# Count stage of a graph network: a block's four fixed tiles get their keys from one 512-column instruction, and their weights from another

## What is computed

```
src, dst = (edge_index[0], edge_index[1])
agg = x + segment_sum(x[src], tgt, num_segments=n)          # layer 0, both directions
h = relu(concat([x_row, x_col - x_row]) @ W1 + b1) @ W2 + b2  # layer 1, segment_max over row
...
comb = dst * num_rel + edge_type                              # layer 3
cnt = segment_sum(ones, comb)
norm = 1.0 / clip(cnt[comb], 1.0)
agg = segment_sum(msg * norm[:, None], dst, num_segments=num_nodes)
```

## Time and profile before

| | us |
|---|---|
| median of 3 runs | 5897.77 (5896.78 to 5898.04) |
| the profiled execution, its own time | 5894.55 |
| span of its core in the trace | 5892.6 |
| count stage, 60 to 731 us of the span | 671 |
| VectorE busy in that stage | 641.5 |
| ScalarE busy in that stage | 269.0 |

### The profile page before, as it was taken

The page is one execution under the profiler, slowest core; times in us unless marked ns, Lnnn a source line. Parts: engine busy times, 40 slices in busy tenths (PEclk is TensorE's granted clock), DMA queues, the critical chain, the costliest instruction groups (busy, mean ns, idle before and its releaser), DMA issues. The chain is left out here.

```text
span 5892.6 us, 107675 instructions
## 1 busy us (share of the span) xinstructions
PE 4004.4 (68%) x31282; PEld 3016.9 (51%) x31283; DVE 3825.4 (65%) x9916; ACT 2230.1 (38%) x2892; POOL 1396.0 (24%) x1703
## 2 busy tenths in 40 slices
PE   4666676635445554445558888888888788878886
PEld 2222276624444444444444444444444488867886
DVE  7999967755655555656534555535555677767776
ACT  2444332001111111111115655545555466646664
POOL 0000000037777777777740000000000000000000
PEclk8999988855555555555558999979999799978998
DMA  1111144522222222222111111111111111111110
GB/s 45 58 67 56 65 175 171 215 61 59 59 59 59 59 59 58 64 58 54 48 33 62 56 56 57 49 51 56 56 56 56 51 46 44 39 36 61 39 44 23
DMA packets 235223, 370.66 MB, mean 63 GB/s; under 512 B 169839, under 2 KB 175973, under 8 KB 235142
## 3 DMA queue, kind: packets, MB, share of 16 engines
q1 hardware_dynamic: 190006, 264.11, 13.8%
q0 software_dynamic: 41536, 85.08, 5.4%
q10 hardware_dynamic: 3600, 20.48, 0.8%
HBM read 292.58 MB, written 76.99 MB: 63 GB/s over the span
## 5 line engine op out<-in xcount | busy, mean ns | idle before, releaser
L1069 POOL DMA_INDIRECT en_got<-edge_q,en_now x1296 | 1302.1, 1005 | 409.4 <-issue 325.1
L1258 PE MATMUL en_t<-ident,en_got 128*128 128x128 f32 x1296 | 361.4, 435 | 957.7 <-DVE en_got L1152 957.7
L1296 ACT ACTIVATE en_hid<-en_t 128x512 f32<-128x512 f32 x324 | 193.5, 597 | 1649.6 <-DMA en_got<-edge_q,en_now 1408.2
L1258 PEld LDWEIGHTS en_t<-ident,en_got 128*128 128x128 f32 x1296 | 231.9, 217 | 1036.1 <-DVE en_got L1152 1036.1
L1266 PEld LDWEIGHTS en_o<-en_w2s,en_hid 128*128 128x128 f32 x2592 | 583.0, 334 | 0.0
L1266 PE MATMUL en_o<-en_w2s,en_hid 128*128 128x64 f32 x2592 | 577.6, 411 | 0.0
L1152 DVE TENSOR_TENSOR en_got<-en_got,p (+1 forms) x324 | 224.5, 693 | 494.7 <-ACTq L1290 462.4
L1855 PE MATMUL r1s_ps<-hp,r1s_count 128*128 128x193 bf16 x5000 | 445.8, 253 | 81.2 <-DVE r1s_count L1807 57.0
L1855 PE MATMUL r0s_ps<-hp,r0s_count 128*128 128x193 bf16 x5000 | 445.6, 253 | 81.4 <-DVE r0s_count L1807 56.2
L456 PE MATMUL cnt_ps<-cnt_hot_l,cnt_hot_k 128*128 128x400 bf16 x1600 | 359.6, 356 | 193.9 <-DVE cnt_hot_l L421 182.0
L1855 PEld LDWEIGHTS r1s_ps<-hp,r1s_count 128*128 128x128 bf16 x5000 | 432.4, 100 | 94.5 <-issue 91.1
(11 more groups left out here) (393 smaller groups left out, 7633.3 us busy)
## 6 DMA issues: line engine op xcount, KB each, us to landing
en_got<-edge_q,en_now POOLq DMA_INDIRECT x1296
count_panels<-cnt_panel SPq DMA_DIRECT2D x25, 800.0 KB, 3.4
type_panels<-cnt_panel SPq DMA_DIRECT2D x25, 800.0 KB, 4.8
c0s_panel<-count_panels SPq DMA_DIRECT2D x25, 800.0 KB, 4.3
count_rows<-c0s_rows ACTq DMA_DIRECT2D x25, 800.0 KB, 3.5
c1s_panel<-count_panels SPq DMA_DIRECT2D x25, 800.0 KB, 5.5
c1s_rows<-count_rows SPq DMA_DIRECT2D x25, 800.0 KB, 7.3
en_raw<-count_panels SPq DMA_DIRECT2D x25, 800.0 KB
```

The costliest lines, as they stand in the source:

```text
L1069: pool.indirect_dma_start(out=got[:, i, j, :], out_offset=None, in_=k.q[:, :], in_offset=bass.IndirectOffsetOnAxis(ap=now[i][:, j:j + 1], ...
L1258: last = pe.transpose(tps[i % 2][:, j * P:(j + 1) * P], got[:, i, j, :], k.ident[:, :])
L1296: act.activation(hid[i % 2][:, :], tps[i % 2][:, :], ACT.Relu).then_inc(lined, 1)
```

## The change

The keys of a block's four fixed tiles are made by one `tensor_tensor` (128 x 4 x 128: `here`, repeated four times, compared with each tile's number from `now`, spread over 128 columns), and their weights by a second (the keys just made, times each tile's power from `now`). Both stand in step 0. The four `lows` remain instructions of their own, two between the two new ones and two in step 1. A semaphore `keyed` orders the second behind the first. Step 0 now waits until both steps of the block before last are used, and step 1 has no such wait. The additional tiles, TensorE, ScalarE and SyncE are as before.

```
-                v.wait_ge(used, w * STEPS + (u * STEPS + s + 1))
-                for j in (2 * s, 2 * s + 1):
-                    last = tile([hot_k[:, u % 2, j, c, :] for c in range(2)], hot_l[:, u % 2, j, :], u,
-                                *(now[u][:, j, c:c + 1] for c in range(3)))
-                last.then_inc(hots, 1)
+                if s == 0:
+                    key_of_all(w, u)
+                else:
+                    for j in (2 * s, 2 * s + 1):
+                        last = low(u, j)
+                    last.then_inc(hots, 1)
...
+            def low(u, j):
+                return v.tensor_scalar(hot_l[:, u % 2, j, :], iota_l[:, :], now[u][:, j, 0:1], None, ALU.is_equal)
+
+            def key_of_all(w, u):
+
+                wide = lambda c: now[u][:, :, c:c + 1].broadcast_to([P, FIX, P])
+                v.wait_ge(used, w * STEPS + (u * STEPS + 2))
+                v.tensor_tensor(hot_k[:, u % 2, :, 0, :], here[u][:, :].unsqueeze(1).broadcast_to([P, FIX, P]), wide(1),
+                                ALU.is_equal).then_inc(keyed, 1)
+                for j in range(FIX // 2):
+                    low(u, j)
+                v.wait_ge(keyed, w + (u + 1))
+                v.tensor_tensor(hot_k[:, u % 2, :, 1, :], hot_k[:, u % 2, :, 0, :], wide(2),
+                                ALU.mult).then_inc(hots, 1)
```

More of the change, by code:

```diff
@@ L379, in count_edges @@
         ps = [ctx.enter_context(nc.psum_tensor(f"cnt_ps{u}", [P, 2 * CUT], F32)) for u in range(SETS)]
-        iotas, own_v, ready, laid, hots, used, more_hots, more_used, copied, stored = map(
-            sem, ("iotas", "own", "ready", "laid", "hots", "used", "more_hots", "more_used", "copied", "stored"))
+        iotas, own_v, ready, laid, keyed, hots, used, more_hots, more_used, copied, stored = map(
+            sem, ("iotas", "own", "ready", "laid", "keyed", "hots", "used", "more_hots", "more_used", "copied", "stored"))
         passed = [sem(f"passed{e}") for e in range(3)]
```

## The result

The changed kernel takes 5917.42 us (median of 7 runs, 5914.59 to 5918.69), the kernel before, run beside it, 5896.89 (7 runs, 5890.73 to 5899.57). The ratio is 1.0035, 95% interval 1.0024 to 1.0047: slower by 20.5 us. The forecast was 5901. The time lies in its range (5882 to 5922), but not in the class held likeliest, no change: over 5909.6 is slower, which had 0.27. The profiled execution has a span of 5915.8 us for 5892.6, 23.2 more.

What follows compares the result with a forecast made beforehand. In the count stage VectorE looked like the bound, the loop through TensorE and ScalarE 0.26 us shorter; after the change that loop binds. Cycles gave -3 us, blocks with two additional tiles +6, together +3: 5901 us, range 5882 to 5922.

Steps and rivals of the forecast that it cites:

- the loop through three engines: Count stage, per pair of blocks: VectorE, TensorE, ScalarE in turn; 5.93 us before, under VectorE's 6.19; 6.01 after, as bound.
- pairs A, B, C and D: Count stage's four block pairs per eight-block cycle: first during a panel store, second often at TensorE's lower clock, others clean.
- VectorE's instructions: Count stage: eight short instructions a block become two of 512 columns, 0.61 us each by starts; VectorE gains 65 us.
- The wait for `keyed`: Count stage, before the weights: keys are done after 0.69 us, weights made at 1.07, two `low` cover it; no cost.
- DVE's register loads: Count stage, one for two blocks: fewer instructions but as much time queued ahead; the first pair waits for ScalarE anyway; no cost.
- The clock: Rival, count stage: TensorE idles in other places, one more even block per cycle falls to lower clock; +22 us, chance 0.15.
- The sum: Count stage: -3 us over 25 cycles of four pairs, +6 from blocks with two additional tiles; together +3 us.
- The DRAIN rule: VectorE's next instruction waits until the pipe is empty; a block would lose 0.86 us, not 0.32; the trace did not agree.

Runs made afterwards that it cites:

- 5: The changed kernel with VectorE's two register loads of each four blocks moved ahead of the wait for `keyed`, the wait kept; 5904.28 us.
- kernel 1: The changed kernel with the second 512-column instruction reading `here` instead of the keys, so without the wait for `keyed` (weights wrong); 5908.80 us.
- two mends: The changed kernel with ScalarE laying a pair before copying the even block ahead, and VectorE's register loads moved ahead of the `keyed` wait; both together 5833.37 us.
- kernel 2: The kernel before plus only a wait: the first tile's key counts `keyed` up, the second tile's `lows` waits for it; 5945.74 us.

## Why the prediction was right and wrong

- **What bounds, the loop through three engines:** right, and the part that carries over. 5.93 us of loop under 6.19 of VectorE was read from the earlier trace rows; the changed loop was worked out at 6.01, and 5 has 6.02 and 6.00. In kernel 1 the pairs A, B, C and D take 7.40, 6.65, 6.02 and 6.05 us in the median, for 7.45, 6.87, 6.01 and 6.01: only B was sized too long. Kernel 1 has a stage of 668.8 where the forecast of +3 gives 672.6.
- **VectorE's instructions:** right. 0.61 from start to start (322.87 to 323.48), 0.69 long; -64 us of busy time for -65.
- **The wait for `keyed`, "no cost":** the step that failed. It was weighed on the engine, where the key is indeed done when its reader starts. The question that was not asked is what the *sequencer* does from when it reaches the wait, which is earlier.
- **"DVE's register loads ... no cost":** failed with it. "As much time" is queued ahead of step 1 only if the sequencer may run ahead through it, and the change took that cover away: 56.8 us of gaps in the blocks and some 28 at their tops, 16 to 18 us on the stage, since ScalarE's loop hides the rest. That pair A waits for ScalarE anyway was a misreading as well: in 23 of 25 pairs A the load was bare by 0.3 us or more already before, under the name of TensorE.
- **The clock:** the rival (one more even block in each cycle, +22 us) would give about this time but is not what happened. The stage's mean clock is 0.95 for 0.94, and 189 matmuls are over 420 ns long, for 217. The slower side came true by a mechanism not among the rivals.
- **Outside the stage:** the forecast had nothing. +5.6 us came from there, by the place of the code.
- **The sum:** +3 forecast; +16.9 in the stage, +5.6 in the edge stage and +0.7 elsewhere are the 23.2 of the profiled spans. The range held because the clock's case had widened it, not because this was foreseen: that is luck. The DRAIN rule, weighed and set aside, stays set aside: L424 starts 0.61 us into the 0.69 of L430. The Trainium skill, page "VectorE: DVE Perf Modes", the same section, itself goes on that an instruction not held starts earlier, which the rows agree with.

## What to carry to other kernels

A wait on an engine's own earlier instruction is free for the engine and not for its sequencer: look what is queued behind it that the sequencer does alone (loads of registers, branches, the head of a loop), and put these ahead of the wait. When an engine's work is shortened, find the loop of waits that comes next and mend it in the same edit: here two mends worth 12 and 16 us alone were worth 90 together, and the change without them was a loss. Before a small gain or loss is believed, compare a stage that the edit does not touch; the place of later code moved one here by 6 to 12 us. And before a wait is believed, look when the releaser named was done: here 4.3 us or more before a wait put down to it ended, and the true cause was the engine's own sequencer.

## What the runs showed of the hardware

- A VectorE sequencer's load of registers from memory takes 0.60 us (594 to 601 ns in the rows above) and up to 1.9 while a panel is stored, and how early it starts depends on the nearest unmet wait ahead of it: with the block before, 1.9 us into it after.
- A wait for a semaphore that VectorE's own instruction counts up held its sequencer: the next register instruction started 0.05 us after that instruction's end, in all 199 blocks.
- A wait that is met when the engine arrives still cost 51 us over 200 blocks (kernel 2), by 50 gaps in front of step 1, 61 us in all and up to 1.9 each, where 23 gaps of 11.5 us stood before.
- A TENSOR_TENSOR of 512 columns with an int16 or bf16 operand beside an fp32 one spread over the columns is 683 to 686 ns long and lets the next start after 0.60 or 0.61: the fp32 rows' price.
- VectorE's gaps in front of the same instruction in unchanged code were 2.7, 5.0, 5.2 or 5.7 us each in the mean, by how many instructions lie ahead of it.
